# State-space block of a small language model: its 192 channels laid out as 128 and 64 rows, and its turn put in another order

## The reference, cut to what matters

```
h = layernorm(x) * ln1_w + ln1_b
z, xBC, dt = h @ in_proj.T                # 384, 512 (= 384 + 64 + 64), 6 columns
xBC = silu(causal_conv4(xBC) + conv_b)    # xs, B, C
dt = softplus(dt + dt_bias); dA = exp(-dt * exp(A_log))
state = state * dA + (dt * xs) outer B    # 6 heads, state 64 x 64; y = state . C + D * xs
y = y * silu(z); y = y / rms(y) * norm_w
x = x + y @ out_proj.T
h2 = layernorm(x) * ln2_w + ln2_b
a, g = h2 @ fc1.T                         # 384 and 384 columns
result = x + (a * silu(g)) @ fc2.T        # added to the residual h of the tower
```

## Time and profile before

| | |
|---|---|
| median of 3 runs | 2194.19 us (2193.48 to 2196.16) |
| the profiled execution, its own time | 2192.55 us |
| its span | 2190.8 us, mean granted PE clock 0.936 |
| PE busy in the span | 1974.5 us (90%) |
| DVE, ACT, POOL busy | 1137.2, 750.8, 428.5 us |
| state-space block | about 927 to 1406 us of the span |

### The profile page before, as it was taken

How to read it: one execution, slowest core, us unless ns; L and a number is a source line. 1 busy time by engine, 2 the same in 40 slices (tenths; PEclk the granted TensorE clock), 3 DMA queues, 4 the chain that set the end, 5 groups by cost and what they waited for, 6 DMA issues and landing times. The chain is left out here.

```text
span 2190.8 us, 27883 instructions
## 1 busy us (share of the span) xinstructions
PE 1974.5 (90%) x10040; PEld 1243.3 (57%) x10048; DVE 1137.2 (52%) x2687; ACT 750.8 (34%) x1251; POOL 428.5 (20%) x526
## 2 busy tenths in 40 slices
PE   4996618999999999679999999699999999999997
PEld 2343513444444444446666665465567888888886
DVE  5798577666666756156677676337411222222221
ACT  1434002555455545355555554121111111111111
POOL 5200100121012201211111111110371222322232
PEclk9988558999999999979999999789999999999999
DMA  2600002121111111000000000200123221222221
GB/s 64 229 34 0 0 13 89 47 61 52 51 37 58 51 51 30 13 14 6 6 6 6 6 6 6 97 2 1 48 77 95 67 59 30 67 60 61 67 36 19
DMA packets 68618, 94.30 MB, mean 43 GB/s; under 512 B 15354, under 2 KB 57630, under 8 KB 66209
## 3 DMA queue, kind: packets, MB, share of 16 engines
q1 hardware_dynamic: 52354, 76.76, 10.9%
q0 software_dynamic: 16128, 15.76, 4.1%
HBM read 54.53 MB, written 39.47 MB: 43 GB/s over the span
## 5 line engine op out<-in xcount | busy, mean ns | idle before, releaser
L972 DVE TENSOR_REDUCE row_max<-c_ps_m 128x1 f32<-128x512 f32 x384 | 252.6, 686 | 115.9 <-PE c_ps_m L1130 110.5
L1308 ACT ACTIVATE e<-c_ps_s 128x512 f32<-128x512 f32 x384 | 216.6, 596 | 222.1 <-PE c_ps_s L1146 221.3
L2593 DVE TENSOR_TENSOR e_f<-e_ps_u,e_gate 128x512 f32<-128x512 f32 x120 | 83.0, 691 | 271.2 <-ACT e_gate L2875 178.7
L2394 POOL DMA_INDIRECT out<-m_o,m_row_of x80 | 125.7, 1571 | 281.5 <-issue 251.6
L2810 PE MATMUL e_ps_o<-m_w,e_f 128*128 128x192 f32 x960 | 162.6, 326 | 0.9 <-DVE e_f L2593 0.9
L1130 PE MATMUL c_ps_m<-c_kT,qT 96*128 96x512 bf16 x384 | 150.3, 398 | 11.0 <-DVE row_max L972 10.9
L2810 PEld LDWEIGHTS e_ps_o<-m_w,e_f 128*128 128x128 f32 x960 | 158.1, 190 | 3.3 <-DVE e_f L2593 1.3
L1146 PE MATMUL c_ps_s<-qT,c_kT 97*128 97x512 bf16 x384 | 145.5, 389 | 12.3 <-ACT e L1308 5.0
L2875 ACT ACTIVATE e_gate<-e_ps_g 128x512 f32<-128x512 f32 x120 | 71.6, 597 | 242.3 <-PE e_ps_g L2784 162.3
L2778 PE MATMUL e_ps_g<-m_xT,m_w 128*128 128x256 f32 x480 | 129.6, 392 | 1.0 <-DVE h L2425 1.0
L2778 PE MATMUL e_ps_u<-m_xT,m_w 128*128 128x256 f32 x480 | 123.2, 379 | 0.0
(11 more groups left out here) (430 smaller groups left out, 3766.2 us busy)
## 6 DMA issues: line engine op xcount, KB each, us to landing
dealt<-x SPq DMA_DIRECT2D x8, 1290.0 KB, 15.1
m_x<-dealt SPq DMA_DIRECT2D x40, 258.0 KB, 2.7
spread<-parts SPq DMA_DIRECT2D x24, 384.0 KB, 2.4
qT<-spread SPq DMA_DIRECT2D x144, 64.0 KB, 2.4
c_kT<-spread SPq DMA_DIRECT2D x144, 64.0 KB, 2.4
m_w<-in_w13e SPq DMA_DIRECT2D x8, 1152.0 KB, 5.3
m_w<-in_w2e SPq DMA_DIRECT2D x8, 576.0 KB, 6.4
out<-h SPq DMA_DIRECT2D x8, 384.0 KB, 4.5
```

What stands on the lines that cost most here:

```text
L972: dve.tensor_reduce(row_max[:, n // J, n % J:n % J + 1], ps_m[:, n % 2, :], AX_X, ALU.max)\
L1308: act.activation(e[:, n % LIVE_E, :], ps_s[:, n % 2, :], ACT.Exp, scale=QSCALE).then_inc(e_ready, 1)
L2394: pool.indirect_dma_start(out=out_rows, out_offset=bass.IndirectOffsetOnAxis(ap=row_of[:, n % 2, r:r + 1], axis=0), in_=o[:, n % 2, r, :], ...
```

## The change

The 192 channels, in the block's inputs and weights, were 2 x 96 rows. Now they are 128 rows (slot 0) and 64 rows (slot 1), and the 64 stand twice, on partitions 0 to 63 and 64 to 127. For that `y` and `y2` are 256 columns wide, the last 64 a copy, and `halves` lays the weights out. PE does several projections as one block: first the 64-row parts, by turns on the lower and the upper row half, then the 128-row parts. The queues are put in another order: z0 is projected with x0 and x1, z1 and z2 with x2 and x3; the turning of x comes ahead of and around that of y2; `apply_2` comes ahead of `norm_1`, `times_dt` ahead of `times_cb`; ACT does conv_silu 1 to 3 ahead of `decay`; the sum h + x2 goes from DVE to POOL, and `rstd_1` of t + 2 between dtx_rest 1 and 2. Nothing else of the kernel changes.

```diff
-        begin(("dt", 0), ("x", 0), ("x", 1), ("x", 2), ("x", 3), ("z", 0), ("sums", 0))
+        begin(("dt", 0), ("x", 0), ("x", 1), ("z", 0), ("x", 2), ("x", 3), ("z", 1), ("z", 2), ("sums", 0))
         end(("sq", 0), ("sq", 1), ("sq", 2), ("sq", 3), ("out", 0), ("out", 1))
         begin(("row", 0), ("row", 1), ("row", 2), ("row", 3), ("row", 4), ("row", 5), ("cb", 0), ("bt", 0),
               ("ec", 0), ("ec", 1), ("ec", 2))
+        begin(("xt", 0), ("xt", 1))
         end(("y2", 0), ("y2", 1))
-        begin(("z", 1))
+        begin(("xt", 2), ("xt", 3))
         end(("g", 0), ("a", 0))
-        begin(("xt", 0), ("xt", 1))
-        end(("g", 1), ("a", 1))
-        begin(("xt", 2), ("xt", 3))
-        end(("g", 2), ("a", 2))
-        begin(("z", 2))
+        end(("g", 1), ("a", 1), ("g", 2), ("a", 2))
...
-        self.lnw = sb("lnw", [CH, 4, 2])
-        self.wz = sb("wz", [CH, 2, ZW])
-        self.wx = sb("wx", [CH, 2, 4 * P])
+        self.lnw = sb("lnw", [P, 4, 2])
+        self.wz = sb("wz", [P, 2, ZW])
+        self.wx = sb("wx", [P, 2, 4 * P])
...
-        y = sb("d_y", [P, J, C])
-        y2 = sb("d_y2", [P, J, C])
-        yT = sb("d_yT", [CH, 2, T])
-        y2T = sb("d_y2T", [CH, 2, T])
+        y = sb("d_y", [P, J, 2 * P])
+        y2 = sb("d_y2", [P, J, 2 * P])
+        yT = sb("d_yT", [P, 2, T])
+        y2T = sb("d_y2T", [P, 2, T])
...
# gpsimd, turn(t)
                     pool.tensor_tensor(rstd2[:, :], var2[:, :], kit.minus_half[:, 0:J], ALU.pow).then_inc(r2_ready, 1)
-                if t + 2 < B:
-                    rstd_1(t + 2)
+                    here = kit.h[:, t * J:(t + 1) * J, :]
+                    pool.tensor_tensor(here, here, x2[:, :, :], ALU.add).then_inc(x2_added, 1)
                 if begins:
                     u = t + 1
                     pool.wait_ge(decays_ready, u + 1)
                     for j in range(J):
+                        if j == 2 and t + 2 < B:
+                            rstd_1(t + 2)
                         pool.wait_ge(by_dve["xt"], count("xt", u, j))
...
# vector, apply_1, add_out, apply_2, add_o, turn(t)
                 for dst, k in ((y, 1), (xm[:, t % 2], 0)):
                     for j in range(J):
-                        last = dve.tensor_scalar(dst[:, j, :], kit.h[:, t * J + j, :], mv1[:, j, 0:1],
-                                                 rstd1[:, k, j:j + 1], ALU.subtract, ALU.mult)
-                    if k == 1:
-                        last.then_inc(y_ready, 1)
+                        dve.tensor_scalar(dst[:, j, 0:C], kit.h[:, t * J + j, :], mv1[:, j, 0:1],
+                                          rstd1[:, k, j:j + 1], ALU.subtract, ALU.mult)
+                dve.drain()
+                dve.tensor_copy(y[:, :, C:2 * P], y[:, :, P:C]).then_inc(y_ready, 1)
...
                     dve.wait_ge(rms_ready, t + 1)
+                    if t > 0:
+                        dve.wait_ge(x2_added, t)
...
-                ln_apply(dve, y2, x2, mv2, rstd2).then_inc(y2_ready, 1)
-
-            def add_x2(t):
-                here = kit.h[:, t * J:(t + 1) * J, :]
-                dve.tensor_tensor(here, here, x2[:, :, :], ALU.add)
+                ln_apply(dve, y2[:, :, 0:C], x2, mv2, rstd2)
+                dve.drain()
+                dve.tensor_copy(y2[:, :, C:2 * P], y2[:, :, P:C]).then_inc(y2_ready, 1)
...
                 dve.wait_ge(w_psum, place[key] + 1)
+                if k == 0:
+                    dve.wait_ge(x2_added, t + 1)
...
                     norm_2(t)
+                if ends:
+                    apply_2(t)
+                if begins:
+                    for j in range(J):
+                        times_dt(u, j)
+                    times_cb(u, 0)
                 if later:
                     norm_1(t + 2)
                 if ends:
-                    apply_2(t)
-                    add_x2(t)
+                    times_gate(t, 0)
                 if begins:
-                    for j in range(J):
-                        times_cb(u, j)
+                    times_cb(u, 1)
+                if later:
+                    apply_1(t + 2)
+                if ends:
+                    times_gate(t, 1)
+                    times_gate(t, 2)
+                if begins:
+                    times_cb(u, 2)
+                    times_cb(u, 3)
                     for j in range(J - 1):
                         times_c(u, j)
-                if later:
-                    apply_1(t + 2)
-                for m in range(KD):
-                    if ends:
-                        times_gate(t, m)
-                    if begins and m < 2:
-                        times_dt(u, 2 * m)
-                        times_dt(u, 2 * m + 1)
...
# tensor: steps, project and hidden are gone; turn_rows turns columns c*P:(c+1)*P of [P, J, 256]
+            row_half = (slice(0, P // 2), slice(P // 2, P))
+            def projections(*keys):
+                for n, key in enumerate(keys):
+                    half, (k, t, i) = row_half[n % 2], key
+                    if k == "dt":
+                        pe.wait_ge(by_act["y"], count("y", t, 1))
+                    if (k, i) == ("g", 0):
+                        pe.wait_ge(by_act["y2"], count("y2", t, 1))
+                    free(key)
+                    if k == "dt":
+                        for j in range(J):
+                            pe.matmul(bank(key)[:, j * NH:(j + 1) * NH], yT[half, 1, j * P:(j + 1) * P],
+                                      wz[half, 1, DI:ZW], start=j == 0, stop=False, skip_group_check=True)
+                    else:
+                        w, col, rows = weights(key)
+                        pe.matmul(bank(key), w[half, 1, col:col + P], rows[half, 1, :], start=True, stop=False)
+                for key in keys:
+                    if key[0] == "dt":
+                        for j in range(J):
+                            last = pe.matmul(bank(key)[:, j * NH:(j + 1) * NH], yT[:, 0, j * P:(j + 1) * P],
+                                             wz[:, 0, DI:ZW], start=False, stop=j == J - 1, skip_group_check=True)
+                    else:
+                        w, col, rows = weights(key)
+                        last = pe.matmul(bank(key), w[:, 0, col:col + P], rows[:, 0, :], start=False, stop=True)
+                    last.then_inc(w_psum, 1)
...
                 if begins:
-                    steps(u)
-                    project("x", u, 0)
-                    project("x", u, 1)
+                    projections(("dt", u, 0), ("x", u, 0), ("x", u, 1), ("z", u, 0))
...
-                    project("x", u, 2)
-                    project("x", u, 3)
-                    project("z", u, 0)
+                    projections(("x", u, 2), ("x", u, 3), ("z", u, 1), ("z", u, 2))
...
+                    turn_x(u, 0)
+                    turn_x(u, 1)
                 if ends:
                     for c in range(2):
                         turn_rows("y2", t, c)
                 if begins:
-                    project("z", u, 1)
-                for m in range(KD):
-                    if ends:
-                        hidden("g", t, m)
-                        hidden("a", t, m)
-                    if begins and m < 2:
-                        turn_x(u, 2 * m)
-                        turn_x(u, 2 * m + 1)
-                if begins:
-                    project("z", u, 2)
+                    turn_x(u, 2)
+                    turn_x(u, 3)
+                if ends:
+                    projections(("g", t, 0), ("a", t, 0))
+                    projections(("g", t, 1), ("a", t, 1), ("g", t, 2), ("a", t, 2))
...
# scalar, turn(t)
+                    conv_silu(u, 0)
+                    z_silu(u, 0)
                     x_copy(u, 2)
                     x_copy(u, 3)
-                    conv_silu(u, 0)
-                    z_silu(u, 0)
+                    z_silu(u, 1)
+                    z_silu(u, 2)
                 if ends:
                     for j in range(J):
                         squares(t, j)
                 if begins:
+                    for i in range(1, 4):
+                        conv_silu(u, i)
                     decay(u)
...
                     affine("y2", t, 1)
-                if begins:
-                    for i in range(1, 4):
-                        conv_silu(u, i)
-                    z_silu(u, 1)
...
-                if begins:
-                    z_silu(u, 2)
```

More of the change, by code:

```diff
@@ L1428, in state_space_block @@
         w_out = sb("w_out", [P, KD, C])
-        wf1 = sb("wf1", [CH, 2, 6 * P])
+        wf1 = sb("wf1", [P, 2, 6 * P])
         wf2 = sb("wf2", [P, KD, C])
@@ L1819, in turn_rows @@
                 for j in range(J):
-                    last = pe.transpose(bank(key)[0:CH, j * P:(j + 1) * P], src[:, j, c * CH:(c + 1) * CH],
-                                        kit.ident[:, :])
+                    last = pe.transpose(bank(key)[:, j * P:(j + 1) * P], src[:, j, c * P:(c + 1) * P], kit.ident[:, :])
                 last.then_inc(w_psum, 1)
```

(46 more changed lines are left out.)

4 lines of the change are left out of this document (2 added, 2 removed).

## The result

Four runs of the changed kernel: 2183.99 us in the median (2181.55 to 2185.66), against 2194.9 (2193.48 to 2196.16) for the kernel before on the same chip: ratio 0.9953, interval 0.9938 to 0.9968. It is faster by 0.5%, 10.9 us; the forecast was 2190 in a range of 2175 to 2206. The profiled execution took 2185.66 us, span 2183.2, mean granted clock 0.932.

What follows compares the result with a forecast made beforehand. PE was taken to set the pace, busy 156.87 of 162 us. The profiled 2192.55 - 14.3 + 9 - 0.5 + 2 = 2188.8, with 1.64 added for the median 2190.4, so 2190 us; range 2175 to 2206.

Steps and rivals of the forecast that it cites:

- turns 0 to 6, without the clock: Seven turns of the state-space block: each gains 2.1 us (53.7 to 51.6), the last a little less, -14.3 us.
- clock in turns 0 to 6: PE's clock falls after y2's wait in five turns instead of two, 5.4 us lost against 3.4: +2 us.
- turn -1: Turn that only begins, one chain: ACT's rows read late, then norm_1, root, apply_1; w_out 8.5 us later, +9 in all.
- turn 7: Last turn: g and a save 1.8 us, apply_2's hold and copy cost 1.9; taken as -0.5 us.
- PE's work: Projections on PE: 64-row passes run side by side, 0.4 us changing over per block; 20.6 us a turn instead of 24.1.
- The chain over ACT: ACT in each turn: conv_silu(3) ahead of decay, so table and rows come late; PE waits 1.1 us for the sixth row.
- The hold by POOL: POOL work starting first holds DVE's tensor_scalars: 1.55 us in apply_2 by the sum h + x2, 1.0 in apply_1 by dtx_rest.
- Rival 1: Nothing is held: adds and dtx_rest don't stop DVE, or DVE comes first; 11 us less, 2179; chance 0.22.
- Rival 2: PE from decay's sixth row to g: clock drops in all seven turns, and in a further stretch; 2206; chance 0.20.
- Rival 4: ACT's chain is shorter than walked, so PE's 3.5 us come through, 4.7 per turn, 2172; chance 0.08.

Runs made afterwards that it cites:

- the swap of the tile: Changed kernel with conv_tile 2 ahead of split_sums on DVE: ratio 0.9882 to the kernel before, turn 49.39 us.
- the run with POOL's work behind: Changed kernel with POOL's sum h + x2 and the root of t + 2 moved behind the four dtx_rest: ratio 0.9924 to the kernel before, turn 50.36 us.
- ACT's order alone: Changed kernel with, in turn -1 only, ACT's decay, rows, cb, b and spread C ahead of conv_silu 1 to 3: ratio 0.9926 to the kernel before.
- the three edits: Changed kernel with conv_tile 2 ahead of split_sums, POOL's sum and root behind dtx_rest, and turn -1 in its own order: ratio 0.9814 to the kernel before.
- the last kernel: The three edits, plus in turn -1 split_sums ahead of conv_tile 2 and times_cb ahead of times_dt: ratio 0.9796 to the kernel before, block 453.3 us.

## Why the prediction was right, step by step

The sign holds: faster, to which the prediction gave 0.45. The size holds only roughly. The sum forecast a gain of 3.8 us and 10.9 came, so the time lies in the range of 2175 to 2206, but at the lower edge of what the forecast called its own, 2184. The mechanism was in the main the one forecast. Its terms:

| term | predicted | measured |
|---|---|---|
| turns 0 to 6, without the clock | -14.3 | -18.4 |
| clock in turns 0 to 6 | +2 | -1.6 |
| turn -1 | +9 | +11.7 |
| turn 7 | -0.5 | -2.5 |
| block | -3.8 | -10.8 |

The first two rows are -20.0 together. The clock is measured by what single turns take beyond the others of their kernel: before, 4.8 us in turn 0 and 1.7 in turns 1 and 4 each, 8.2; after, 6.6 in turn 0. Three terms erred to one side and turn -1 to the other, so that the sum is 7.0 us off and not 9.7; that part is luck.

*PE's work.* Right. Passes side by side, 0.2 us at each changing over (a block of eight halves takes 1.91 instead of 1.72, and the eight whole passes behind it 1169.35 - 1165.81 = 3.54 instead of 3.43), the second block 5.45 us (5.55 predicted), g and a 1195.14 - 0.16 - 1186.39 = 8.59 (8.5). Only the first block was 6.05 and not 6.5: dt's small passes on the lower half and x0's on the upper overlap, which I had left out. On one half the same passes take 1.3 us more, where the pair of x1 and z0 alone explains 0.9.

*The chain over ACT.* Right: the row is waited for 0.98 us (1.1 predicted), y2's affine 0.45, and the swap of the tile shows that these waits hang on conv_tile 3. A turn came out at 51.0, 51.6 predicted; the 0.3 added for what the walk on the kernel before left open was not needed, and the other 0.3 to 0.4 is about the first block. Over seven turns these 0.6 us make the 4.1 of the first row.

*The hold by POOL.* Right in place and size: apply_2 takes 2.73 us (1.24 + 1.55 predicted), apply_1 1.0 more. Rival 1 is refuted by the run with POOL's work behind, where the hold goes. (The prediction calls all of rows 9 adds; L329 is a product.) The Trainium skill ("SBUF — State Buffer", "Who interferes with whom") has the engine that issues first holding the shared pair for its whole instruction, and the other fully blocked. The trace agrees for the sum: POOL was 0.07 us ahead, and the first tensor_scalar ended with it. That these 0.07 us decided it is not shown, since in no run DVE came first. By itself the hold is worth 3.8 us in the block. Rival 1 had priced it at 11, since it took 1.3 us a turn to come through where ACT lets 0.6.

*The clock.* The term that was wrong in sign. I took five falls behind y2's wait instead of two, +2 us; it came to -1.6. In the kernel before the clock was at 1.2 GHz at the start of turn 0, behind y2's wait in turns 0 and 4, and once more in turn 1, a fall that the prediction does not name (windows of the kernel before: length, busy, clock):

```profile
1034.50:1041.50 7.00, 7.00 (x28) 0.76 0.00 0
1172.10:1179.10 7.00, 5.79 (x40) 1.00 0.01 2
```

The first is the first block of turn 1: PE is busy all the time, and has had no pause since y2's wait in turn 0. The second is the place in turn 3 at which the window of the earlier trace rows stands in turn 4, with the same instructions and the same busy time, at full clock. After the change none of these three falls was there, but the stretch at 1.2 GHz at the start of turn 0 was longer, behind PE's waits of 9.69 and 1.90 us: turn 0 cost 6.6 us more than a later one, before 4.8. So it gained 0.9 us where a steady turn gains 2.7. Rival 2 is refuted: turns 1 to 6 ran without a fall in all nine profiles of the new order that have the pairs on both halves or no pairs. With all halves on one side it fell once, in turn 2, behind a wait of 0.99 us (0.76 over 1140 to 1147 us). What tells a wait that drops the clock from one that does not stays open, since the same instructions with the same wait dropped it in one turn and not in another, and no run isolates it. For the old order there is one profile with each of the two layouts of rows, so it is not shown either that its falls are gone for a reason.

*Turn -1.* Right in sign, 2.7 short. The norm_1, root, apply_1 that stand behind times_dt made the long wait, as the walk had it. Two things were missing. The first rows of y come 1.5 us later, since the signal now stands behind xm and the copy, 14.76 us of wait instead of 13.24; I had counted neither here. And behind PE's wait of 4.49 the clock was at 1.2 GHz when x was turned, 2.77 us instead of the 1.51 of the run with the tile first. Those two make 2.8. The text named the late rows on ACT first; ACT's order alone is worth 2.3 us of it.

*Turn 7.* -2.5 instead of -0.5, but this turn alone scatters by 2.4 us between profiles that don't touch it. Part of it runs at the lower clock, where the passes of g0 and a0 take 4.7 us instead of 3.0.

*Rival 4* did not come: the waits were there. Its 4.7 us per turn appear with the three edits, when the waits are worked away (53.7 - 48.9 = 4.8).

## What to carry to other kernels

Walk all queues of one turn with measured durations before you trust a count of PE's passes: the rows shorten a turn of the new order by 3.6 us, but the whole change gained 2.7, since that order brings waits of its own. They lay in one chain, and a swap of two lines on DVE took 1.6 back. Treat the first and the last turn of a software pipeline as stages of their own; an order that is right for the steady turn cost 11.7 us in the one that only begins. And start long elementwise work on POOL where DVE has no tensor_scalar due.

## What the runs showed of the hardware

- A wait's price can be three times its length: with the 2.04 us for the state in turn 0 the first block took 6.8 us longer, since the clock fell within the wait and the passes then ran at 1.2 GHz (one comparison, three edits against the last kernel).
- A root on POOL (pow on 128x8, 1.70 us) held none of the three tensor_scalars of DVE that started beside it, where an add of 128x768 held exactly the first of four: 2.73 us together instead of 1.25. So the rule of the first engine does not hold for every POOL instruction.
- Products of two SBUF operands on both engines seem to take turns: in the three edits one times_cb, started 0.20 us behind the third dtx_rest, took 1.45 us instead of 0.95, and the fourth dtx_rest, started while it ran, 1.54 instead of 0.83. That they wait for each other's end is read from these times and not tested.
- 64-row passes of two different jobs with different widths (6 columns on the lower, 512 on the upper half) overlap too: x0's first pass starts at 1151.05, among the eight of dt, and all 64-row passes of the first block take 2.38 us, on one half 3.67.
